# Keeping the next iteration's packed expert word in VectorE's register instead of reading it twice

## The reference, cut to what matters

```
# gelu mixture, on the normalised x
logits = (x @ gate_w + gate_b) / 0.9
gate_probs = softmax over the 2 largest of 8 logits, 0 elsewhere
h = gelu(x @ w1[e] + b1[e])              # 128 -> 512
out = sum over e of gate_probs[e] * (h @ w2[e] + b2[e])
x = x + 0.5 * (layernorm(out) * ln_g + ln_b)

# swiglu mixture, on the normalised x
h = silu(x @ w1[e].T) * (x @ w3[e].T)    # 128 -> 256
out = sum over the 2 chosen e of weight[e] * (h @ w2[e].T)
x = x + 0.5 * out
```

## Time and profile before

| | |
|---|---|
| runs | 1291.59, 1292.12, 1297.62 us |
| median | 1292.12 us |
| profiled execution | 1289.35 us |
| its span, first to last instruction | 1287.6 us |
| mean granted TensorE clock | 0.908 |

### The profile page before, as it was taken

How to read it: one execution, slowest core, us unless ns; L and a number is a source line. 1 busy time by engine, 2 the same in 40 slices (tenths; PEclk the granted TensorE clock), 3 DMA queues, 4 the chain that set the end, 5 groups by cost and what they waited for, 6 DMA issues and landing times. The chain is left out here.

```text
span 1287.6 us, 28074 instructions
## 1 busy us (share of the span) xinstructions
PE 1006.0 (78%) x6835; PEld 849.4 (66%) x6836; DVE 877.7 (68%) x3115; ACT 599.5 (47%) x1746; POOL 746.8 (58%) x721
## 2 busy tenths in 40 slices
PE   2599999477466999978788794598789874599893
PEld 2499999444255999978787794244344444589892
DVE  5655678577783666786577564689969967466763
ACT  0256777556323667755344353351345131245562
POOL 2787458720047566775757666266635734767555
PEclk9999999787858999999899897799999985799997
DMA  7745345200012333322233342000000000334353
GB/s 233 229 135 135 105 138 150 67 1 0 0 48 72 101 100 93 105 83 86 93 102 93 99 132 80 6 1 1 0 1 0 0 0 17 95 112 127 102 148 108
DMA packets 146194, 102.92 MB, mean 80 GB/s; under 512 B 16324, under 2 KB 134934, under 8 KB 146070
## 3 DMA queue, kind: packets, MB, share of 16 engines
q1 hardware_dynamic: 70530, 39.35, 10.6%
q0 software_dynamic: 16384, 33.59, 8.7%
q10 hardware_dynamic: 59156, 28.57, 7.6%
HBM read 52.44 MB, written 49.02 MB: 79 GB/s over the span
## 5 line engine op out<-in xcount | busy, mean ns | idle before, releaser
L595 PE MATMUL gelu_hb<-gelu_xsT,gelu_weights 128*128 128x128 f32 x2208 | 303.8, 283 | 2.5 <-issue 2.5
L595 PEld LDWEIGHTS gelu_hb<-gelu_xsT,gelu_weights 128*128 128x128 f32 x2208 | 279.9, 199 | 3.0 <-issue 2.7
L692 ACT ACTIVATE gelu_hid<-gelu_hb,gelu_weights 128x128 f32<-128x128 f32 x736 | 209.1, 375 | 122.2 <-PE gelu_hb L595 90.4
L1232 POOL DMA_INDIRECT slots_x<-gelu_xn,gelu_index x176 | 175.4, 996 | 94.4 <-issue 45.7
L606 PE MATMUL gelu_ob<-w,gelu_hid 128*128 x1472 | 196.4, 277 | 3.9 <-DVE gelu_ys L974 3.5
L606 PEld LDWEIGHTS gelu_ob<-w,gelu_hid 128*128 128x128 f32 x1472 | 180.5, 194 | 5.2 <-issue 5.2
L986 DVE COPY gelu_weights<-w 128x516 f32 x184 | 87.0, 490 | 64.5 <-issue 35.2
L1908 POOL TENSOR_TENSOR rwkv_tw<-rwkv_tw,rwkv_qr 128x512 f32<-128x512 f32 x64 | 79.5, 1273 | 54.0 <-DVE rwkv_tw L1867 44.9
L595 PE MATMUL swiglu_hb<-swiglu_xsT,swiglu_weights 128*128 128x128 f32 x736 | 100.3, 281 | 0.0
L974 DVE TENSOR_TENSOR gelu_ys<-gelu_ob,bias 128x128 f32<-128x128 f32 x184 | 49.5, 287 | 71.1 <-PE gelu_ob L606 68.1
L595 PEld LDWEIGHTS swiglu_hb<-swiglu_xsT,swiglu_weights 128*128 128x128 f32 x736 | 92.3, 198 | 0.0
(11 more groups left out here) (382 smaller groups left out, 2108.6 us busy)
## 6 DMA issues: line engine op xcount, KB each, us to landing
gelu_xs<-slots_x SPq DMA_DIRECT2D x69, 256.0 KB
slots_y<-gelu_ys ACTq DMA_DIRECT2D x138, 128.0 KB
swiglu_xs<-slots_x SPq DMA_DIRECT2D x23, 256.0 KB
slots_y<-swiglu_ys ACTq DMA_DIRECT2D x46, 128.0 KB
raw_s<-in_L_ffn_w ACTq DMA_DIRECT2D x12, 256.0 KB
slots_x<-zeros SPq DMA_DIRECT2D x2, 1472.0 KB, 10.4
slots_x<-gelu_xn,gelu_index POOLq DMA_INDIRECT x176, 2.4
w<-in_L_ffn_w SPq DMA_DIRECT2D x1, 2048.0 KB, 13.8
```

Of the source, the lines that this page charges most:

```text
L595: last = pe.matmul(hb[j][:, c * P:(c + 1) * P], weights[:, odd * BODY + j, c * P:(c + 1) * P], xsT[j // SET][:, j % SET, :], start=True, s ...
L692: last = act.activation(hid[:, j % RING, c * P:(c + 1) * P], hb[j][:, c * P:(c + 1) * P], ACT.Gelu, bias=weights[:, odd * BODY + j, FF + c ...
L1232: pool.indirect_dma_start(slots_x[:, :], bass.IndirectOffsetOnAxis(index[p][:, k, g:g + 1], 0), tokens[p][:, g, :], None).then_inc(sent[p] ...
```

## The change

`words_of` of VectorE keeps the last word that it read, under the number of the iteration that it belongs to. If the next call is for that iteration and the number is a Python integer, the kept register is used as its first word, and only the following words are read. In a loop, and for the first iteration, all words are read as before. TensorE's and ScalarE's reads are not touched.

```diff
+            following = {}
+
             def words_of(i, turns, _then):
 
-                return [word_at(i + n) for n in range(turns + 1)]
+                known = following.pop(i, None) if isinstance(i, int) else None
+                words_now = [word_at(i) if known is None else known] + [word_at(i + n) for n in range(1, turns + 1)]
+                following.clear()
+                if isinstance(i, int):
+                    following[i + turns] = words_now[turns]
+                return words_now
```

## The result

The changed kernel takes 1287.76 us (median of 9 runs, 1282.04 to 1288.84), the kernel before 1293.77 (9 runs, 1291.59 to 1297.74). The ratio is 0.9946 with a 95% interval of 0.9927 to 0.9965: 7.0 us faster, 4.5 to 9.4. The forecast was 1287.8 by a gain of 4.3 us from a lower median; the gain was larger, and the experiments show a part of where.

A forecast was written before the change was run, and what follows sets the result against it. No single engine fills the span; VectorE's word reads cost only where its queue is empty and someone waits. Gains 0 + 1.22 + 3.06, say 4.3 us, from median 1292.12 gave 1287.8 us, range 1285.5 to 1290 (8 in 10: 1283.0 to 1293.5).

The forecast's parts named there:

- The number of reads, 95 (71 and 24): VectorE's line 979: 184 reads fall to 95, 71 in gelu-named tiles and 24 in the last mixture.
- First mixture, 0: 10 to 264 us: 22 reads less gain 0, since TensorE waited for nobody but 0.2 us.
- Second mixture, 1.22: 348 to 811 us: 45 reads less gain 0.59 in the gelu half plus 0.63 in the swiglu half.
- The two late places of the gelu half: VectorE's copies at 463.67 and 474.36 us: two reads worth 1.26, of which 0.59 counted, TensorE's loss at 478.31.
- The wait at 658: TensorE's wait of 2.13 us in the swiglu half: to become about 1.5, a gain of 0.63.
- The cover at 722: TensorE's 7.65 us wait for GpSimd's transfers absorbs two reads, 1.26 us, and grows by about 1.3.
- Third mixture, 3.06: 1064 to 1287 us: five places pay, the first 0.54 us and the other four 0.63 each.
- The stretch at low clock: 3.40 us at clock 0.50 from 1146.80 us: costs 1.5 us, might come back, left out of the sum.
- The sum, 4.3: Whole kernel: gains of the three mixtures, 4.28 us, say 4.3; this forecast had chance 0.53.
- the chain taken at its word: Rival: covers at 478 and 722 fail, ten read pairs pay 6.3 plus 1.5 for clock, 7.8 us: 1284.3; chance 0.22.
- Slower: longer low-clock stretches: Rival: TensorE waits longer for GpSimd and the clock stays low longer: 1292.9, up to 1297 us; chance 0.08.
- a sign of being wrong: Whole kernel: low-clock stretches that come or go would show the prediction wrong.

The follow-up runs named there:

- only_third: The changed kernel with the word kept in the third mixture only, the others reading twice; against the kernel before: 1287.86 us, ratio 0.9946.
- only_second: The changed kernel with the word kept in the second mixture only, the others reading twice; against the kernel before: 1290.76 us, ratio 0.9962.
- before_again: The kernel before, unchanged, profiled once more in a later series: 1536.67 us in one run, beside a median of 1534.83 of 24 runs.

## Why the prediction was right, and where its steps were not

- **The number of reads, 95 (71 and 24):** exact, and by it the kept word costs no instruction. The idle time in front of the copies fell by 0.70 and 1.16 us at the places of rows 5 and by 0.68 and 0.69 at those of rows 12, to 0.41 to 0.73: a read is worth its pitch and a little more. Of TensorE's waits of rows 13 the first and the last are gone and the others went from 0.78, 1.29 and 0.79 to 0.17, 0.71 and 0.28, each by 0.5 to 0.6; of the later ones around 0.5 us, such as that at 1201.19, some stay.
- **First mixture, 0:** this step failed. "TensorE waited for nobody but 0.2 us" was read as "TensorE loses nothing". It lost 1.67 us, most of it in steps too short for the view, and loses 0.0 after (0.84 and 1.27 in the two other profiles with both reads). Iteration by iteration 0.9 us of gain appear in three steps (0.20, 0.34 and 0.35 us, ahead of iterations 5, 10 and 11, in both profiles of the changed kernel) which neither only_third nor only_second has; by the durations of the whole stage it is 1.2 to 2.6 us against the profile of before, and more against only_second (254.4) and only_third (255.3).
- **Second mixture, 1.22:** not confirmed as a sum. The two late places of the gelu half, put at 0.59, gave 1.2 to 1.4 in iterations 10 to 17, but 1.46 us went the other way before iteration 4. The bracket of 0.59 at 478 was itself short by 0.16: there the first matmul comes 1.64 us after the start of the group of eight before it, where 0.89 is undisturbed, a loss of 0.75. The other 0.43 stands at a place left out. The swiglu half stays unresolved in its scatter, and the cover at 642 us, which the prediction did not name, stands in it. The wait at 658 went to 1.78 and 1.50 was expected.
- **The cover at 722:** confirmed. TensorE gained before it and waited longer there (7.65 to 10.26, and 10.04 in the second profile; expected: longer by 1.3), because GpSimd's run did not get shorter. Only_second has 10.73, and only_third, with its reads there, 7.54. Of the 2.6 us more in the first profile 0.6 are GpSimd's own run, which took that much longer; the rest, 2.0, is TensorE's earlier arrival after the start of that run. It is more than the 1.3 expected. A stretch of 6.8 us at 0.50, at 703 us before and at 709 in only_third, is absent from all three profiles without these reads and may be the difference.
- **Third mixture, 3.06:** a term mis-sized. It was 5.0 to 5.2 where like is compared with like: 3.4 in bracketed waits, 0.75 in what the brackets leave out, and 0.95 in short steps at places that "TensorE's own work hides". The sentence that no wait of TensorE for the multiplication follows behind the other pairs was also a misreading: there are three before, of 0.51 (at 1211), 0.29 (1251) and 0.32 us (1265), of which the second is gone after. The stretch at low clock, named and left out of the sum, was rightly left out. That what TensorE gains reaches the end whole held but for 0.2 to 0.4 us.
- **The sum, 4.3:** 7.0 and 10.0 were measured. That the absolute time agrees so well with the forecast (1287.76 and 1287.8) is luck: the median of three runs that it started from was 1.5 us below that of the 27 runs, and the gain was put too small by 2.7 us. In size the gain is that of the rival "the chain taken at its word" (7.8), but not by its mechanism: the cover that this rival denied is there, and what made up the difference are losses that neither of them counted.
- **"Slower: longer low-clock stretches":** it did not happen, but low-clock stretches came and went, which the prediction had named as a sign of being wrong. Within the second mixture TensorE spent 97.8 us at 0.50 before, 106.9 in the first profile of the changed kernel, whose stage is 5.2 us longer, and 97.8 again in the second, whose stage takes 461.9. Only_third, with its reads there, has 112.7. So the time at low clock moves with and without the change, and the medians are well clear of it.

## What to carry to other kernels

A wait that the profile does not show is not a wait that is not there: where matmuls follow one another at a pitch well below their record's length, compare the starts of equal groups with the undisturbed pitch, and do it before a stage is costed at nothing. A sequencer's register read costs its pitch (0.63 us here) only where its engine's queue is empty, so price it place by place, and expect each further read to cost more than the last one removed brings (92 more: 23 us, 89 fewer: 7 to 10). And price a stage from several profiles: here one stage moved by 5 us between two executions of one kernel, more than the whole forecast. Before a low-clock stretch that is gone is put down to a change, look for it in a profile that lacks the change at that place; here it was gone there too.

## What the runs showed of the hardware

The same kernel before took 1293.6 us in one series of runs and 1534.8, 1536.1 and 1559.1 in the three later ones, each time in all of its runs (the lowest of the 15 in the last series was 1550.07). It was not one chip's: the first and the last series name the same chip. In before_again the state-space layer (84.2 us) and the receptance layer (253.0) are as long as ever; all of the excess is in the mixtures (305.8, 583.9 and 298.2 us). Inside the first mixture 33.7 us are lost between the starts of iterations 0 and 10, while iterations 11 to 15 start 7.58 us apart in both conditions, to within 0.01 us. What grows is idle time that nothing in the profile explains; the mean durations change little. TensorE's first product in the kernel before and in before_again:

```profile
L595 PE MATMUL gelu_hb<-gelu_xsT,gelu_weights 128*128 128x128 f32 x2208 | 303.8, 283 | 2.5 <-issue 2.5
```

```profile
L595 PE MATMUL gelu_hb<-gelu_xsT,gelu_weights 128*128 128x128 f32 x2208 | 330.0, 296 | 31.2 <-issue 28.6 <-DVE gelu_weights L986 1.9 <-ACT gelu_hid L692 0.7
```

The mean of 296 as against 283 ns goes with more time at the lower clock (mean granted 0.855 as against 0.908). Two of the expectations above take it for granted that the instructions arrive late wherever iterations are written out. No run shows that, and the traces speak against so simple a rule. By the branches of line 486, TensorE runs iterations 8 to 11 and 13 to 18 of the first mixture as loops, while VectorE and ScalarE have no loop in it. Yet the looped iterations 8 and 17 take 9.75 and 9.84 us in before_again as against 7.58 and 7.59, and iteration 12, written out on all three, takes 7.59 as against 7.58. No run changed the amount of code with the work kept the same, so the cause stays open. The change is worth about the same share under both conditions (0.9923 and 0.9946, and 0.9934).
